# MoE gates turned on VectorE in 32x32 blocks instead of by transposes on TensorE, with ScalarE copying the second 64 rows

## The reference

```python
def _L1_ffn_ref(x, A, B, Wr):            # x: the output c of the masked linear map
    xf = x.reshape(-1, x.shape[-1])      # 1024 tokens, 512 features
    scores = xf @ Wr.T                   # 64 expert scores for each token
    top_vals, top_idx = jax.lax.top_k(scores, 16)
    gates = jax.nn.softmax(top_vals, axis=-1)
    G = jnp.zeros((N, K), xf.dtype).at[jnp.arange(N)[:, None], top_idx].set(gates)
    h = jnp.einsum('nd,krd->nkr', xf, A) # 64 experts of rank 16: 1024 hidden values for each token
    out = jnp.einsum('nkr,kdr->nd', h * G[:, :, None], B)
    return out * 2.0
```

## Time and profile before

| what | value |
|---|---|
| median of 3 executions | 355.08 us (354.74 to 355.09) |
| the profiled execution's own time | 354.69 us |
| its span, first to last instruction | 353.0 us |
| PE busy | 349.5 us, 99% of the span |
| PEld busy | 294.4 us, 83% |
| DVE busy | 202.2 us, 57% |
| ACT busy | 144.1 us, 41% |
| POOL busy | 78.0 us, 22% |
| granted TensorE clock | full in all 40 slices of the page |

### The profile page before, as it was taken

One profiled execution on the slowest core, in us unless ns is written; L12 is line 12 of the kernel. 1 busy time (PEld: TensorE's weight loads), 2 busy tenths in 40 slices (PEclk: granted clock), 3 DMA queues, 4 the chain that ended last, 5 costly groups with the idle time before them and its releaser, 6 DMA issues.

```text
span 353.0 us, 4621 instructions
## 1 busy us (share of the span) xinstructions
PE 349.5 (99%) x1682; PEld 294.4 (83%) x1682; DVE 202.2 (57%) x302; ACT 144.1 (41%) x196; POOL 78.0 (22%) x86
## 2 busy tenths in 40 slices
PE   8999999999999999999999999999999999999997
PEld 8899888888888888888888898888888888888885
DVE  3788755334533453685674565879888878501102
ACT  5577544422442243545464471566352443201100
POOL 2361657863340004000000000000041154002200
PEclk9999999999999999999999999999999999999999
DMA  7943343232120054297219019010052022101011
GB/s 202 323 126 144 114 138 112 78 104 77 52 80 0 0 177 130 79 395 291 59 35 306 3 22 417 38 52 11 0 177 62 0 61 69 51 32 59 30 61 59
DMA packets 14802, 37.31 MB, mean 106 GB/s; under 512 B 2272, under 2 KB 4224, under 8 KB 13504
## 3 DMA queue, kind: packets, MB, share of 16 engines
q1 hardware_dynamic: 11920, 31.18, 25.9%
q0 software_dynamic: 2432, 5.57, 5.5%
q10 hardware_dynamic: 432, 0.33, 0.3%
HBM read 34.97 MB, written 2.10 MB: 105 GB/s over the span
## 4 chain that ended last, share of the span: by engine, by line
PE 99%; DVE 0%; issue 0%
PE ps L1157 29%; PE ps L1158 29%; PE ps L1159 29%; PE ps L1179 3%; PE ps L1309 3%; PE ps L1399 1%; PE ps L1386 1%; PE ps L1194 1%; PE ps L1187 1%; PE ps L1198 1%; PE ps L1202 1%; PE ps L1234 1%; PE ps L1408 0%; PE ps L1417 0%; DVE x L1149 0%
## 5 line engine op out<-in xcount | busy, mean ns | idle before, releaser
L1158 PE MATMUL ps<-x_hl,w_hl 128*128 128x512 f32 x144 | 56.2, 390 | 0.0
L1157 PE MATMUL ps<-x_hl,w_hl 128*128 128x512 f32 x144 | 56.2, 390 | 0.0
L1159 PE MATMUL ps<-x_hl,w_hl 128*128 128x512 f32 x144 | 56.1, 389 | 0.0
L462 POOL TENSOR_TENSOR am_hl<-am_raw,am_hl 128x512 fp32r<-128x512 f32 x8 | 11.0, 1387 | 137.4 <-ACT am_hl L479 137.4
L418 POOL DMA_INDIRECT b_raw<-b_gu,row_of x32 | 32.1, 1003 | 27.7 <-DVE b_st L780 19.6
L800 DVE TENSOR_TENSOR glu<-glu,ps 128x512 f32<-128x512 f32 (+1 forms) x22 | 14.9, 683 | 38.8 <-ACT glu L511 26.0
L1159 PEld LDWEIGHTS ps<-x_hl,w_hl 128*128 128x128 f32 x144 | 27.1, 188 | 5.7
L511 ACT ACTIVATE glu<-ps 128x512 f32<-128x512 f32 (+1 forms) x22 | 12.8, 588 | 46.0 <-PE ps L1179 45.8
L1157 PEld LDWEIGHTS ps<-x_hl,w_hl 128*128 128x128 f32 x144 | 27.1, 188 | 5.4
L1158 PEld LDWEIGHTS ps<-x_hl,w_hl 128*128 128x128 f32 x144 | 27.1, 188 | 5.2
L1158 PE MATMUL ps<-act,wd_hl 128*128 128x512 f32 x80 | 31.2, 390 | 0.0
(11 more groups left out here) (151 smaller groups left out, 729.0 us busy)
## 6 DMA issues: line engine op xcount, KB each, us to landing
wc_raw<-mask_w SPq DMA_DIRECT2D x8, 1024.0 KB, 7.0
w_raw<-w_gu SPq DMA_DIRECT2D x8, 512.0 KB, 3.3
wd_raw<-w_dn SPq DMA_DIRECT2D x10, 256.0 KB, 2.7
w_raw<-w_t SPq DMA_DIRECT2D x2, 1024.0 KB, 7.3
x<-x_blocks SPq DMA_DIRECT2D x2, 1024.0 KB, 6.3
am_raw<-a_moe SPq DMA_DIRECT2D x8, 256.0 KB, 2.8
bm_raw<-b_moe SPq DMA_DIRECT2D x4, 512.0 KB, 3.6
x_raw<-x_blocks SPq DMA_DIRECT2D x7, 256.0 KB, 6.7
```

The lines of the kernel that those rows point to most:

```text
L462: nc.gpsimd.tensor_tensor(am_hl[:, j % AM_SLOTS, 1], am_raw[:, j % 2], am_hl[:, j % AM_SLOTS, 0].bitcast(F32), ALU.subtract).then_inc(am_l ...
L1157: nc.tensor.matmul(out, w_high, m_high, start=start, stop=False)
L1158: nc.tensor.matmul(out, w_high, m_low, start=False, stop=False)
L1159: return nc.tensor.matmul(out, w_low, m_high, start=False, stop=stop)
```

## The change

VectorE now scales all four token blocks with one `scalar_tensor_tensor` into `gate_tok` (64 gates a token, once), and turns them itself with eight `transpose` instructions a half: each takes 32 partitions (32 tokens of each of the four token blocks) by 4 x 32 gates and writes 32 experts by 4 x 32 tokens into rows 0 to 63 of `gate_x`. ScalarE copies rows 0 to 63 of `gate_x` to rows 64 to 127. `turn_gates` is gone from TensorE, with its two places in the order. `combine` waits for both gate copies from the start.

```diff
+BLOCK = 32
-        gate2 = at("gate2", [P, 4, 2, EXPERTS], F32, R_ACT + 54 * KB)
+        gate_tok = at("gate_tok", [P, 4, EXPERTS], F32, R_ACT + 54 * KB)
         gate_x = at("gate_x", [P, 2, HALF], F32, R_AD)
...
             def gate_copy(s):
-                act_e.wait_ge(gate_tr, s + 1)
-                copy(gate_x[:, s], ps[:, 6]).then_inc(late_banks_free, 2)
+                act_e.wait_ge(gate_turned, s + 1)
+                copy(gate_x[EXPERTS:P, s], gate_x[0:EXPERTS, s]).then_inc(late_banks_free, 2)
...
                 step(nc.vector.tensor_reduce(gate_sum[:], left1[:], AX_X, ALU.add))
                 step(nc.vector.reciprocal(gate_inv[:], gate_sum[:]))
-                if s:
-                    dve.wait_ge(gate_tr, s)
-                for t in range(4):
-                    last = nc.vector.tensor_scalar(
-                        gate2[:, t], left1[:, t].unsqueeze(1).broadcast_to([P, 2, EXPERTS]),
-                        gate_inv[:, t:t + 1], MOE_SCALE, ALU.mult, ALU.mult)
-                last.then_inc(gate_done, 1)
+                step(nc.vector.scalar_tensor_tensor(gate_tok[:], left1[:], MOE_SCALE,
+                                                    gate_inv[:].unsqueeze(2).broadcast_to([P, 4, EXPERTS]),
+                                                    ALU.mult, ALU.mult))
+                for e in range(0, EXPERTS, BLOCK):
+                    turned = gate_x[e:e + BLOCK, s].rearrange("p (t q n) -> p t q n", t=4, n=BLOCK)
+                    for q in range(P // BLOCK):
+                        last = nc.vector.transpose(turned[:, :, q],
+                                                   gate_tok[q * BLOCK:q * BLOCK + BLOCK, :, e:e + BLOCK])
+                last.then_inc(gate_turned, 1)
...
-            def turn_gates(s):
-                pe.wait_ge(gate_done, s + 1)
-                if s:
-                    pe.wait_ge(late_banks_free, 2)
-                for t in range(4):
-                    last = nc.tensor.transpose(ps[:, 6, t * P:t * P + P],
-                                               gate2[:, t].rearrange("p c e -> p (c e)"), ident)
-                last.then_inc(gate_tr, 1)
-
...
             turn_scores(1)
-            turn_gates(0)
             pe.wait_ge(ct_lo, BATCH)
             experts(2)
             experts(3)
             experts(4)
             experts(5)
-            turn_gates(1)
             for n in range(6, 2 * JT):
                 experts(n)
...
                 for s in range(2):
-                    pe.wait_ge(late_banks_free, 2 * o + s + 1)
+                    pe.wait_ge(late_banks_free, max(4, 2 * o + s + 1))
                     pe.wait_ge(hg_lo, HALF_TAIL + AM_SLOTS * s)
```

More of the change, by code:

```diff
@@ L233, in build @@
         s_ready, s_copied, score_ready = sem("s_ready"), sem("s_copied"), sem("score_ready")
-        top_step, shifted, exp_done, gate_done = sem("top_step"), sem("shifted"), sem("exp_done"), sem("gate_done")
-        gate_tr, late_banks_free = sem("gate_tr"), sem("late_banks_free")
+        top_step, shifted, exp_done = sem("top_step"), sem("shifted"), sem("exp_done")
+        gate_turned, late_banks_free = sem("gate_turned"), sem("late_banks_free")
         am_hi, am_lo, h_ready, hg_mul, hg_hi, hg_lo = (sem("am_hi"), sem("am_lo"), sem("h_ready"), sem("hg_mul"),
```

## The result

The changed kernel takes 355.46 us (median of 22 executions, 355.18 to 356.18) against 354.94 for the kernel before beside it (22, 354.33 to 355.75): ratio 1.0017, 95% interval 1.001 to 1.0023. It is slower by 0.6 us by the ratio (0.4 to 0.8; the medians differ by 0.52), and so by less than the 0.2% that was set as the bound of no difference. The forecast was 355.4, or +0.34.

What follows compares the result with a forecast made beforehand. TensorE, busy 99% of the span, was taken as the bound: 0.83 us saved there, outweighed by stalls from VectorE's 3.32 us lateness, gives +0.34, or 355.4 us against the median of 355.08; range 354.1 to 356.5.

Steps and rivals of the forecast that it cites:

- The saving on TensorE: Dropping both turn_gates from TensorE's chain saves 0.45 - 0.06 + 0.44 = 0.83 us.
- A transpose's step: VectorE's eight transposes a half don't overlap and take 0.31 us from start to start; bounds 0.20 and 0.43.
- the rival of a dearer transpose: A VectorE transpose costs more than a plain instruction on 128 elements: T = 0.335, +0.74 us, 355.8; chance 0.22.
- The scaling in half 0: VectorE's single scaling, beside GpSimd's subtractions, ends between 266.01 and 266.45; taken as 266.35.
- VectorE's lateness: VectorE is 1.17 us late after half 0; half 1 adds 2.15, so hg_gate(3) is 3.32 us late.
- ScalarE behind it: Behind hg_high(3), the gate copy and am_high(4) follow at 0.53 us spacing, making am_high(4) 2.79 us late.
- TensorE's waits: TensorE stalls 0.73 us before experts(7); the first weight load of experts(8) then comes 0.34 us later than before.
- the prediction's general sum: The end moves by the larger of -0.83 and 16T - 4.62 us (1.64, and 2.98); T = 0.31 gives +0.34.
- The late loads: Rival: tile 6's load takes 4.2 us, delaying experts(10) by 0.85 more, 356.3; chance 0.08.
- The `max(4, ...)` of `combine`: Waiting for both gate copies costs nothing, since they ended by 280.16 and combine comes behind all of experts.
- The number: The whole kernel's time: +0.34 us, 355.03 from the execution's own 354.69, or 355.4 against the median of 355.08.

Runs made afterwards that it cites:

- the kernels in which no stall is left: Changed kernel with all transposes on partitions 0 to 31: 354.12 us, ratio 0.9975; changed kernel with two moves of order: 353.99 us, ratio 0.9974.
- two moves of order: Changed kernel, product 3 before half 1's gates on VectorE, tiles 4 and 5's high parts before the second gate copy on ScalarE: 353.99 us, ratio 0.9974.
- the run with sixteen: Changed kernel with sixteen transposes in each half instead of eight, the first eight into a spare tile: 362.64 us against 354.84.

## Why the prediction was right

*The saving on TensorE* (0.83): right. The matmul in front of `experts(7)` stood before at

```profile
281.85 0.39 PE L1159 MATMUL ps<-c_hl,am_hl 128*128 128x512 f32 x1
```

and stands at 281.18 now: 0.67 earlier, and 0.87 without the offset. (With 0.87 the two stalls leave +0.54 instead of +0.58.) Twice the transposes cost 1.0 (0.6 to 1.3), and the kernels in which no stall is left gain 0.9.

*A transpose's step* (0.31, not overlapped): right, 0.315, and for the reason given, as the same instructions on the same partitions take 0.205. One alone takes 0.301 us, 0.01 over the 0.29 worked out for 128 elements, which is what the prediction had taken for filling a block, and close to the 311 ns that was quoted with it; the rival of a dearer transpose fell with it.

*The scaling in half 0* (end at 266.35): it took 0.73 us, where half 1's took 0.42, and ended at 266.51, or 266.31 without the offset.

*VectorE's lateness* (3.32 us): product 3 ended at 282.03 for 278.43, 3.60 and without the offset 3.40. The 0.08 is what sixteen steps make that are each 0.005 longer.

*ScalarE behind it*: here a term was too small. The spacing of 0.53 was taken from copies that stay on the same partitions; a copy from rows 0 to 63 to rows 64 to 127 stands 0.65 behind the instruction in front, and the next 0.66 behind it. That is 0.25 us, so tile 4 was 0.33 later than forecast, with the 0.08 above.

*TensorE's waits* (a weight load 0.73 late, then 0.34 later than before): two stalls at the two places named, of 0.85 and 0.56. The sum came out at +0.58 for +0.34. The weight load of `experts(8)` is 0.67 later than before (285.44 for 284.57, less the offset), as 0.34 and 0.33 make it, but behind the wait the weight load and its matmul start together (285.44 and 285.47), so that the stream of matmuls lost some 0.1 less than the loads. The second wait was released by GpSimd's low part, as forecast. In the prediction's general sum the 2.98 is put down to `am_low(4)`; it is VectorE's lateness, of which 0.53 is the gate copy's gain and 2.45 what `am_low(4)` may be late. The sum is the same.

*The late loads*: tile 6's low part was made from 288.85 to 290.15, with no wait of TensorE behind it; the rival did not come about.

The `max(4, ...)` of `combine` cost nothing: no wait stands there.

*The number.* The mechanism and both places were right. That the forecast of 355.4 lies within 0.1 us of the measured 355.46 is partly luck: the three executions it started from had a median of 355.08, 0.14 above the 354.94 of the 22 beside the changed kernel. The difference was +0.34 for a measured +0.5 to +0.6, and most of what was missing is ScalarE's 0.25.

## What to carry to other kernels

Work moved off the bounding engine is paid back when the engine that takes it over feeds the same chain in written order: list what is queued behind the new work, and set each delay against the slack of its reader, the time by which it may come late before the reader waits. Here 3.4 us of lateness met about 2.6 us of slack in front of `experts(7)` (281.85 - 278.43, less the 0.83 by which TensorE comes earlier), and two moves of order gave the whole gain back, 0.9 us. An instruction that starts on other partitions than the one before it must be priced without overlap, on ScalarE as well as on VectorE; a spacing read from neighbours on the same partitions is too short.

## What the runs showed of the hardware that was not expected

- ScalarE's copies did not overlap where the output's rows changed (from row 0 to row 64, and back): 0.65 and 0.66 us from start to start with instructions of 0.63 us, and 0.53 with all of them on rows from 0 on.
- TensorE's granted clock fell to half for about 3 us behind waits of 4.0 and 2.7 us, beginning some 1.3 and 0.5 us after the matmuls had started again (near 288.2 and 285.4), while it stayed at 1.00 behind the wait of 1.40 us of the run with sixteen, and behind the waits of 0.6 and 0.3 us of the changed kernel. Of the four executions with twelve transposes one kept the full clock; why that one did stays open.
